# Two squares moved ahead of two residual additions in GpSimd's order

## The reference, cut to what matters

```
def mamba2(x, Win, conv_w, conv_b, dt_bias, A_log, D, gnorm, Wout):
    zxbcdt = x @ Win                       # z, xBC, dt
    xBC = silu(conv over 4 positions of xBC)
    dt = softplus(dt + dt_bias);  dA = exp(dt * -exp(A_log))
    h_t = dA_t * h_(t-1) + xdt_t B_t;  y_t = h_t C_t
    y = (y + D * xs) * silu(z)
    return rmsnorm(y, gnorm) @ Wout
x = x + mamba2(rmsnorm(x, norm), ...)
```

## Time and profile before

| what | value |
| --- | --- |
| median of 3 runs | 1198.49 us (1197.13 to 1199.32) |
| profiled execution, from its first to its last instruction | 1202.9 us |
| PE busy | 1042.5 us, 87% |
| DVE busy | 930.2 us, 77% |
| ACT busy | 796.8 us, 66% |
| POOL busy | 301.7 us, 25% |
| mean granted TensorE clock | 0.970 |

### The profile page before, as it was taken

How to read it: one execution, slowest core, us unless ns; L and a number is a source line. 1 busy time by engine, 2 the same in 40 slices (tenths; PEclk the granted TensorE clock), 3 DMA queues, 4 the chain that set the end, 5 groups by cost and what they waited for, 6 DMA issues and landing times. The chain is left out here.

```text
span 1202.9 us, 46297 instructions
## 1 busy us (share of the span) xinstructions
PE 1042.5 (87%) x19940; PEld 539.3 (45%) x19940; DVE 930.2 (77%) x1380; ACT 796.8 (66%) x1512; POOL 301.7 (25%) x306
## 2 busy tenths in 40 slices
PE   4889888988889888898888998889887678999998
PEld 2445444544545454455544555445444422333332
DVE  5789877898788888789887898879888646675654
ACT  3777678777787777777787777777776223333332
POOL 8422132422323123232242322323222200000000
PEclk9899999999999999999999999999999578999999
DMA  3100111101111011010110101101001100000000
GB/s 71 49 15 13 22 32 31 34 3 31 32 31 34 2 32 31 19 44 5 32 31 21 44 4 32 32 18 47 22 14 49 37 1 0 1 10 9 1 10 9
DMA packets 72753, 28.74 MB, mean 24 GB/s; under 512 B 59816, under 2 KB 68328, under 8 KB 72552
## 3 DMA queue, kind: packets, MB, share of 16 engines
q1 hardware_dynamic: 72552, 25.80, 8.7%
HBM read 9.98 MB, written 1.05 MB: 9 GB/s over the span
## 5 line engine op out<-in xcount | busy, mean ns | idle before, releaser
L1501 DVE TENSOR_TENSOR em<-em,gs 128x1536 f32<-128x1536 f32 (+1 forms) x192 | 311.0, 1639 | 9.7 <-ACT em L1139 9.2
L1139 ACT ACTIVATE em<-ring 128x512 f32<-128x512 f32 x480 | 249.0, 598 | 26.2 <-PE ring L858 21.7
L878 PE MATMUL ybank<-em,xdt 64*32 64x64 f32 (+1 forms) x12288 | 181.4, 238 | 32.5 <-issue 30.0
L878 PEld LDWEIGHTS ybank<-em,xdt 64*32 64x32 f32 x12288 | 151.6, 106 | 94.8 <-issue 63.7
L617 POOL TENSOR_TENSOR ysq<-yg 128x512 f32<-128x512 f32 x96 | 140.8, 1467 | 156.8 <-DVE yg L1521 156.8
L858 PE MATMUL ring<-rt,lt 128*64 128x512 bf16 x960 | 148.8, 400 | 18.7 <-ACT em L1139 10.4
L1335 ACT ACTIVATE em<-ring 128x512 f32<-128x512 f32 x128 | 69.5, 594 | 134.4 <-PE ring L1001 134.3
L1737 DVE TENSOR_TENSOR em<-em,ring 128x512 f32<-128x512 f32 x128 | 82.1, 684 | 64.2 <-ACT em L1335 57.6
L624 POOL TENSOR_TENSOR x_t<-on,x_b 128x256 f32<-128x256 f32 x48 | 46.1, 961 | 252.0 <-DVE on L1529 252.0
L1508 DVE SCALAR_TENSOR_TENSOR yt<-xs,col,ybank 128x256 f32<-128x256 f32 x192 | 83.0, 472 | 29.1 <-PE ybank L878 29.0
L624 POOL TENSOR_TENSOR x_b<-on,x_b 128x256 f32<-128x256 f32 x48 | 39.6, 825 | 247.1 <-DVE on L1529 247.1
(11 more groups left out here) (206 smaller groups left out, 1685.1 us busy)
## 6 DMA issues: line engine op xcount, KB each, us to landing
x_b<-x_t SPq DMA_DIRECT2D x48, 128.0 KB
cm<-bc SPq DMA_DIRECT2D x24, 224.0 KB, 2.7
rt<-lt SPq DMA_DIRECT2D x120, 24.0 KB
cw<-in_L_conv_t_cw SPq DMA_DIRECT2D x6, 320.0 KB
cw<-in_L_conv_b_cw SPq DMA_DIRECT2D x6, 320.0 KB, 3.2
x_in<-in_x SPq DMA_DIRECT2D x4, 256.0 KB, 3.4
out<-x_in SPq DMA_DIRECT2D x8, 128.0 KB, 1.9
win<-in_L_conv_t_Win SPq DMA_DIRECT2D x12, 74.0 KB
```

Source lines behind the costliest of these rows:

```text
L878: mm = pe.matmul(ybank[QUAD * q:QUAD * (q + 1), ab, to:to + hi - lo], xdt[m % 2][rows, 8 * (i % 2) + 4 * first + q, r, :], em[rows, p % EM ...
L1139: emptied(act.activation(em[:, p % EM_SLOTS, :, HALF * j:HALF * (j + 1)], o.rearrange("p (h t) -> p h t", h=HEADS), ACT.Exp), "seg", n, i, ...
L1501: dve.tensor_tensor(e, e, gs[n % 2][:, i:i + 1, 0:wide].to_broadcast([P, HEADS, wide]), ALU.mult).then_inc(s_w, 1)
```

## The change

In GpSimd's loop over the blocks the square of couple 1 goes ahead of the addition of couple 0, and the square of couple 2 ahead of the addition of couple 1. Nothing else is changed: the same instructions with the same operands and the same semaphores.

```diff
                 if k:
                     add_x(k - 1, 3)
                 square_y(k, 0)
+                square_y(k, 1)
                 add_x(k, 0)
-                square_y(k, 1)
+                square_y(k, 2)
                 add_x(k, 1)
-                square_y(k, 2)
                 if k % 2 == 0 and k >= 2 and pass_of(k) + 1 < NPASS:
                     weights_made(pass_of(k) + 1)
                 add_x(k, 2)
```

## The result

The changed kernel takes 1214.33 us in the median of 4 runs (1213.22 to 1215.27), the kernel before 1198.9 (1197.13 to 1199.37). The ratio is 1.013, with a 95% interval of 1.0116 to 1.0145: 15.4 us slower. The forecast was 5.0 us slower, or 1203.5, with a range from 1188 to 1214; the measured median lies just above it. The direction was right, the size was a third of what came.

What follows compares the result with a forecast made beforehand. TensorE (busy 87%) and VectorE (77%) were taken as the busiest, GpSimd mattering only through who waits for it. Sum: -7.4 - 2.5 + 21.9 - 7 = +5.0 us, 1203.5 as a median, range 1188 to 1214.

Steps and rivals of the forecast that it cites:

- Edit 1: Couple 1's square ahead of couple 0's addition: `project_out(k,1)` starts earlier, -7.4 us over 23 blocks, -2.5 in the last block.
- Edit 2, the mechanism: Couple 1's addition falls behind weigh 6, delaying ScalarE's `square_x(k+2,0)` by 1.9 or 1.5 us per block, 37.8 us in all.
- Rival A: At GpSimd's back-to-back square and sum, couple 1's addition gets in before weigh 6: 1190 us; chance 0.20.
- Edit 2, the cover: ScalarE's delay partly hidden: its waits ahead of `rstd_of` leave 21.9 us, TensorE's issue stalls swallow 7 more.
- first cover: ScalarE's waits for grams or mean square ahead of `rstd_of` hide 9.9 us in kind 0, 6.0 in kind 1.
- B: Issue stalls and ScalarE's waits swallow 28 of the 37.8 us delay, couple 1's gain stands: 1198.5 us; chance 0.18.
- D: Couple 1's square disturbs nobody (-17.9 us), ScalarE's delay as forecast: -5.5 us, 1193; chance 0.12.
- C: Nothing is swallowed by stalls and couple 1's square pushes weigh 5 by all of itself: +19.4 us, 1218; chance 0.12.

Runs made afterwards that it cites:

- e1: Kernel before with only the square of couple 1 ahead of the addition of couple 0 on GpSimd: 1188.12 us, ratio 0.9915.
- e10: Kernel before with both square moves, ScalarE's `square_x(k+2,0)` behind the silus of z, and VectorE's `finish_dt` ahead of `gate_y(k,1)`: 1177.93 us, ratio 0.982.
- e4: Kernel before, GpSimd's order unchanged, with only ScalarE's `square_x(k+2,0)` moved behind the four silus of z: 1203.05 us, ratio 1.0043.
- e7: Kernel before with an idle ScalarE copy of 1536 columns ahead of `square_x(k+2,0)` in 22 blocks: 1221.6 us, ratio 1.0178.
- e8: The kernel before, unchanged, run again for a second profile: 1198.81 us, ratio 0.9994; the profiled execution spanned 1196.3 us.
- e2: Kernel before with only the square of couple 2 ahead of the addition of couple 1 on GpSimd: 1226.33 us, ratio 1.0235.
- e11: Kernel before, GpSimd's order unchanged, with only VectorE's `finish_dt` moved ahead of `gate_y(k,1)`: 1200.58 us, ratio 1.0013.
- e5: Kernel before with couple 1's square ahead of couple 0's addition and VectorE's `finish_dt` ahead of `gate_y(k,1)`: 1177.14 us, ratio 0.9805.

## Why the prediction was right or wrong

**Edit 1: right.** Forecast -7.4 - 2.5 = -9.9 us, measured -10.1 in e1 (interval 7.8 to 12.7). Each part shows: line 1430 goes from 0.29 to 1.03 us and line 1453 from 1.03 to 0.29; `sum_dt` waits 0.41 us; the third stretch of e1 is 7.1 us shorter in 21 blocks (2.7 of it come back ahead of `rstd_of` in that execution, which is about what two executions of one kernel differ by there); the last block gives 1.8.

**Edit 2, the mechanism: right.** The addition of couple 1 was forecast to end 0.6 us behind weigh 6, with 1.9 us of delay for `square_x` in kind 0 and 1.5 in kind 1, 37.8 in all. Measured are 35.0 us in 21 blocks, and 1.86 for the 22nd: 36.9. ScalarE shows 2.04 and 1.64 us of wait (its 0.18 of before among them). Rival A, the addition getting in first, is out: it took 2.24 us. The forecast let the whole wait at `project_out(k,2)` go (0.64 and 0.31 us); 0.31 us of it stay, for line 803. That the rest is worth nothing, as the forecast costed it, is not shown (e10 and e4).

**Edit 2, the cover: wrong, and this is the step that failed.** The forecast let TensorE's stalls for issue swallow 7 us ("I take 4.5 for the first three and a third of the rest, 2.5: 7 us"). With edit 2 alone, the stretch in which they lie, from `rstd_of` to the next `project_x`, is not shorter but 0.5 us longer, and with both edits it is 1.5 us longer than with edit 1 alone. The dose in e7, without GpSimd, has 4.2 more. Two profiles of the kernel before differ by 2.3 us in this stretch, which is too little to hide the 7. The stalls over 0.2 us in this stretch sum to 16.8 us before (e8) and 16.8 in e2: nothing was swallowed there. They stand at an instruction and not at a time. In block 9 the stall within the pairs 0 and 1 stood at 438.30 with 1.63 us before, behind the 94th product; after, with these products 7.3 us later (435.42 and 442.70), it is there again, behind the 94th:

```profile
445.31 0.54 PE L878 MATMUL ybank<-em,xdt 64*32 64x64 f32 x34 [1.35 <-issue]
```

Some stalls did go. In the lists of waits they sum to 39.3 us before (e8), 27.0 in e2 and 22.0 with both edits. For line 878 the lists of e8 and of e2 have:

```profile
PE ybank L878 <- issue: 28.9, 28, 2.2
```
```profile
PE ybank L878 <- issue: 20.0, 23, 2.1
```

Most of this, 10.5 of the 12.3 us in e2, lies between `square_x` and `rstd_of`: 16.6 us before, 6.1 in e2, 3.7 with both. There TensorE now waits for ScalarE (`gram`, 22.4 us in e2), and a stall beside such a wait no longer shows. But these are the stalls that ScalarE waits for just ahead of `rstd_of` (in the second profile 1.81 us of stall and 1.44 of wait in k=3, 2.17 and 1.93 in k=6), so what they give is in the first cover and can't be counted a second time.

That first cover, ScalarE's waits ahead of `rstd_of`, was set at 15.9 us and gave 7.4 in e2 (9.5 with both edits). Two reasons can be seen. The waits were larger in the profiled execution that was summed: those that end on TensorE's work come to 15.3 us when they are summed again, and to 13.0 in the second profile. And not all of them go: 4.7 us are left in e2. A part of these comes from TensorE's clock. In k=9 of the changed kernel the stretch even grew by 0.38 us: `mean` now waits 0.71 us for the first gram to be copied and runs at a lower clock (2.04 instead of 1.12 us), and ScalarE waits 0.56 us for it.

The two covers were set at 22.9 us together and gave 6.9 in e2 (7.4 - 0.5). Edit 2's term was +14.9; with edit 1's -9.9 it gave +5.0. It measured 28.2 alone and 25.5 on top of edit 1, and 25.5 - 10.1 is the 15.4 of the result.

**The clock, which the forecast left out.** In the blocks from 50 us to the last `project_x` there are 4 places in the first profile of the kernel before and 3 in the second where the granted clock is about 0.6 over 4 us. There are 6 in the changed kernel, 7 in e7 and 9 in e2, but also 7 in e11, which is no slower by its runs: the count varies from one execution to the next. Over whole runs the granted clock is 0.968 in the median of e2, against 0.976 for the kernel before on the same chip. The difference is worth at most 0.008 of the span, 10 us of the 28. Block by block it is less: where such a place falls between `square_x` and `rstd_of`, and the block had no wait to give, the stretch is 0.39 us longer (k = 9 and 14 with both edits). The nine places of e2 would make up to 3.5 us by that, an estimate; what they cost behind `rstd_of` is not separated. In k = 9 the lower clock follows TensorE's new waits; that it comes of them everywhere is not shown.

**Against which time.** The first profiled execution lay 6.6 us above what the second one spans, and the sum was made from its rows. Profile against profile the change is 8.4 us, median against median 15.4. The forecast was carried over to the median as if the execution were a typical one, and noted only that it was 0.4% longer.

**The rivals.** B needed 28 us to be swallowed and D an undisturbed line 1430; both are out. C's 1218 is nearest to the measured time, but by luck: its +21.9 for edit 2 is too small by 4 to 6 us, and it had nothing from edit 1 in the blocks before the last, which is wrong by some 8 us the other way.

## What to carry to other kernels

Before an instruction is put in front of another in an engine's queue, look up who waits for the one that is passed, not only who waits for the one that is brought forward: 0.9 us of room (the sum at 423.15, `square_x` at 424.04) was all that ScalarE had. Where GpSimd and VectorE both read SBUF, the order in which they ask is part of the schedule: the same square costs 0.74 us in each block beside line 1430; behind weigh 5 it holds nobody (the addition behind it then costs line 1451 0.45 us), and moving the VectorE pair of instructions away brought 11 to 13 us more. A stall seen at one place in one execution is no cover for a delay: let it count only if a dose on the delayed engine shows that it does, and count it once, either as TensorE's stall or as the wait that another engine has for it. And when a variant holds a second move, run that move alone before pricing the first: e10 can't price edit 2, because e4 showed a cost in its helper.

## What the runs showed of the hardware that was not expected

TensorE's clock falls for some us inside the blocks. In block 9 of the changed kernel the view by stretches (us, busy and instructions per engine, granted clock, transfers) has, after TensorE's waits of 1.12 and 0.71 us:

```profile
433.00:436.00 3.00, 1.88 (x128) 1.68 (x128) 0.00 (x1) 2.85 (x6) 0.00 (x0) 1.00 0.06 15
436.00:440.00 4.00, 3.62 (x14) 1.83 (x16) 2.58 (x6) 2.90 (x7) 1.76 (x2) 0.57 0.00 0
```

A granted clock of 0.57 is the lower level, 1.2 GHz, for most of the 4 us, and the four transposes of line 847 at 438.22 take 1.06 us instead of 0.66. The kernel before has such places too, one of them after a stall of 1.06 us at 501.7:

```profile
502.00:506.00 4.00, 4.00 (x59) 1.95 (x38) 2.33 (x5) 2.48 (x6) 1.44 (x2) 0.58 0.03 8
```

It has 4 and 3 of them in its two profiles, the changed kernel 6 and edit 2 alone 9. One of them holds back at most 0.43 x 4 = 1.7 us of TensorE's work, and a delay of 1 us in front of TensorE can so cost more than itself.

A VectorE instruction with one input can be held by GpSimd too. Line 1451, a cast from SBUF to SBUF, takes 0.33 us in block 9 of the kernel before and 0.78 in e5 (404.41), where GpSimd's addition starts just ahead of it (404.38); it ends 0.08 us behind the addition. Line 1474, with one input from SBUF and one from PSUM, is not held (0.68 us both ways).

Executions of one kernel differ by some us in TensorE's stalls for issue: 44.0 and 39.3 us in the two profiles of the kernel before, with spans of 1202.9 and 1196.3.
